# A routed-experts block without its last stage: base rows sorted beside the shared expert, finished rows scattered by the blocks

## The reference

```python
x = x + ga * attn(h)                                   # x3 in the kernel
h = _layernorm(x) * (1 + cb) + sb
logits = h @ w_router.T                                # 16 experts, top 1
masked_inputs = sigmoid(top logit) * h                 # to the chosen expert alone
gate, up = split(masked_inputs @ gate_up_proj[e])      # 128 -> 2 x 256
expert_out = (up * silu(gate)) @ down_proj[e]          # 256 -> 128
shared = (silu(h @ w_gate.T) * (h @ w_up.T)) @ w_down.T
x = x + gb * (shared + expert_out)
```

## Time and profile before

| | |
|---|---|
| median of three runs | 394.68 us (393.13 to 394.87) |
| profiled execution | 393.6 us, its span 391.8 us |
| busy: PE, DVE, ACT, POOL | 296.8, 244.0, 179.3, 187.6 us (76, 62, 46, 48% of the span) |
| mean granted clock of the tensor engine | 0.858 |
| chain that ended last, by engine | PE 30%, DVE 24%, POOL 21%, issue 13%, ACT 7%, DMA 3% |
| DMA | 28,184 packets, 25.22 MB, mean 64 GB/s |

### The profile page before, as it was taken

How to read it: one execution, slowest core, us unless ns; L and a number is a source line. 1 busy time by engine, 2 the same in 40 slices (tenths; PEclk the granted TensorE clock), 3 DMA queues, 4 the chain that set the end, 5 groups by cost and what they waited for, 6 DMA issues and landing times.

```text
span 391.8 us, 4364 instructions
## 1 busy us (share of the span) xinstructions
PE 296.8 (76%) x1140; PEld 171.7 (44%) x1140; DVE 244.0 (62%) x514; ACT 179.3 (46%) x436; POOL 187.6 (48%) x267
## 2 busy tenths in 40 slices
PE   4363667877668766877795586699989999999844
PEld 4223234334433534544453343334436666666532
DVE  5148596997989889789688342634335444444423
ACT  2541654947556666555372543222214444444300
POOL 4542726558678485656273534310003666666610
PEclk9956598996998888767889598699999999999955
DMA  6688000102011010010010100132002222222057
GB/s 182 175 241 321 28 0 4 51 0 60 22 47 35 0 54 29 0 41 21 0 49 8 41 14 14 50 97 49 0 1 56 75 75 82 71 77 71 4 155 274
DMA packets 28184, 25.22 MB, mean 64 GB/s; under 512 B 3682, under 2 KB 21734, under 8 KB 28160
## 3 DMA queue, kind: packets, MB, share of 16 engines
q1 hardware_dynamic: 24480, 18.57, 16.5%
q0 software_dynamic: 2528, 4.27, 3.4%
q10 hardware_dynamic: 1152, 2.10, 1.4%
HBM read 17.42 MB, written 8.49 MB: 66 GB/s over the span
## 4 chain that ended last, share of the span: by engine, by line
PE 30%; DVE 24%; POOL 21%; issue 13%; ACT 7%; DMA 3%; SPq 0%; POOLq 0%; DVEq 0%; ACTq 0%
PE bank L858 23%; POOL y_rows L423 11%; PE bank L862 5%; DVE work L524 4%; POOL sorted_rows L400 4%; POOL work L377 3%; ACT work L724 2%; DMA work<-y_rows 2%; DVE work L543 2%; DVE work L519 2%; DVE work L517 1%; DVE work L541 1%; PE bank L901 1%; POOL work L381 1%; DVE work L528 1%
## 5 line engine op out<-in xcount | busy, mean ns | idle before, releaser
L423 POOL DMA_INDIRECT y_rows<-work x47 | 46.2, 982 | 71.2 <-ACT work L838 41.9
L862 PE MATMUL bank<-ident,work 128*128 128x128 f32 x192 | 40.2, 362 | 52.9 <-ACT work L724 23.9
L862 PEld LDWEIGHTS bank<-ident,work 128*128 128x128 f32 x192 | 29.9, 185 | 75.0 <-ACT work L724 28.9
L858 PE MATMUL bank<-up_experts,work 128*128 x94 | 48.2, 595 | 0.0
L685 DVE COPY work<-bank 128x256 f32<-128x256 f32 x47 | 19.9, 424 | 37.7 <-PE bank L1043 37.7
L400 POOL DMA_INDIRECT sorted_rows<-rows,slot_i x32 | 36.5, 1140 | 14.4 <-issue 8.9
L858 PE MATMUL bank<-work,Fk 128*128 128x512 f32 x64 | 34.9, 652 | 5.7 <-DVE work L506 5.7
L724 ACT ACTIVATE work<-work 128x128 f32<-128x128 f32 x64 | 26.3, 487 | 23.5 <-POOL work L381 23.5
L375 POOL TENSOR_SCALAR work<-work 128x4 f32<-128x4 f32 x32 | 6.7, 210 | 59.5 <-DVE work L432 58.6
L377 POOL TENSOR_TENSOR work<-work,neghalf 128x4 f32<-128x4 f32 x32 | 33.2, 1038 | 2.7
L858 PE MATMUL bank<-work,Fv 128*128 128x512 f32 x64 | 33.3, 648 | 0.0
(11 more groups left out here) (161 smaller groups left out, 630.4 us busy)
## 6 DMA issues: line engine op xcount, KB each, us to landing
up_experts<-in_gate_up SPq DMA_DIRECT2D x2, 2048.0 KB, 11.7
work<-sorted_rows SPq DMA_DIRECT2D x47, 66.0 KB, 1.8
work<-in_x SPq DMA_DIRECT2D x8, 256.0 KB, 3.4
work<-in_xT SPq DMA_DIRECT2D x8, 256.0 KB, 3.1
work<-y_rows SPq DMA_DIRECT2D x8, 256.0 KB, 4.2
out_t<-work ACTq DMA_DIRECT2D x8, 256.0 KB, 3.9
sorted_rows<-pad_row SPq DMA_DIRECT2D x17, 66.0 KB, 1.6
y_rows<-work POOLq DMA_INDIRECT x47
```

The costliest lines, as they stand in the source:

```text
L423: pool.indirect_dma_start(y_rows, bass.IndirectOffsetOnAxis(number[q], 0), yb[q], None, bounds_check=NB * T - 1, oob_is_err=False).then_in ...
L858: return pe.matmul(out, w, x, start=start, stop=stop)
L862: last = pe.transpose(out[:, j * P:(j + 1) * P], src[:, j * P:(j + 1) * P], ident[:])
```

## The change

The gates gb are turned into rows with one row for all partitions (gb_rows): eight products against the identity matrix before the main loop, two ScalarE copies, and four transfers that put them into the second 128 columns of `rows`. A sorted row so carries h, gb and the number (260 values instead of 132). GpSimd makes one copy of the down weights per batch, multiplied by gb (`scale_down`, 128 x 256), after each batch's scatter. ScalarE keeps x3 as rows (from the transpose that the norm reads), `shared_down` multiplies in the other orientation (eight matmuls of 128 columns) so that its result is rows, and `shared_base` adds x3. GpSimd scatters these base rows into `sorted_base`, in the experts' order (32 indirect DMAs). Pads of both tensors are written, with a spare number each, behind the tensors' ends, and copied or written at each expert's end.

In the blocks, SyncE loads the sorted rows and the base rows of each block; the first three loads of rows stand ahead of the wait for the base scatters (C_out). Numbers, gate times result, and the addition of the base are VectorE's (`expert_y`, signal D_y); the copy of aT moves from VectorE to ScalarE; the buffers are 8 deep instead of 6. GpSimd scatters finished rows to out_t, which now is tokens by channels with spare rows at its end. The last stage is gone.

```diff
-    ROW = C + 4
+    ROW = 2 * C + 4
+    NUM = 2 * C
     ROOM = NB * T + P
     PADS = E * ROOM
-    NOROW = NB * T
+    SPARE = NBLK - NTT
     LAG = 3
-    DEPTH = 6
-    ENDS = 4
+    DEPTH = 8
+    LEAD = 3
...
+        x3_rows = sb("x3_rows", [P, NB, T])
+        gb_rows = sb("gb_rows", [P, NB, C])
+        Wd_gb = sb("Wd_gb", [P, NB, FC, C])
...
+            sp.wait_ge(K_gb.sem, K_gb.after(0))
+            for j in range(NT):
+                sp.dma_start(rows[:].rearrange("p (b j) r -> p b j r", j=NT)[:, :, j, C:2 * C], gb_rows[:]).then_inc(L_gb.sem, 16)
...
+            pads = sorted_rows[PADS:, :].rearrange("(k p) r -> p k r", p=P)
+            sp.dma_start(pads[:, :, 0:NUM], pad_row[:].rearrange("p (o r) -> p o r", o=1).broadcast_to([P, SPARE + E, NUM])).then_inc(L_pads.sem, 16)
+            sp.dma_start(pads[:, :, NUM:], pad_id[:]).then_inc(L_pads.sem, 16)
+            sp.dma_start(sorted_base[PADS:, :].rearrange("(k p) c -> p k c", p=P),
+                         pad_row[:, 0:C].rearrange("p (o c) -> p o c", o=1).broadcast_to([P, SPARE, C])).then_inc(L_pads.sem, 16)
...
-                sp.dma_start(sorted_rows[bass.ds(at_row, P), :], pad_row[:]).then_inc(L_pads.sem, 16)
+                sp.dma_start(sorted_rows[bass.ds(at_row, P), :], sorted_rows[PADS + (SPARE + e) * P:PADS + (SPARE + e + 1) * P, :]).then_inc(L_pads.sem, 16)
+                sp.dma_start(sorted_base[bass.ds(at_row, P), :], pad_row[:, 0:C]).then_inc(L_pads.sem, 16)
...
+            def load_rows(j):
+                q = j % DEPTH
+                at_row = block_row(j)
+                if j >= DEPTH:
+                    sp.wait_ge(D_y.sem, D_y.after(j - DEPTH))
+                sp.dma_start(xb[q], sorted_rows[bass.ds(at_row, P), :]).then_inc(D_x[q].sem, 16)
...
+            for j in range(LEAD):
+                load_rows(j)
+            sp.wait_ge(C_out.sem, C_out.after(NB - 1))
             for j in range(NBLK):
...
+                if block_no(j + LEAD):
+                    load_rows(j + LEAD)
+                load_base(j)
...
+            def scale_down(b):
+                if b == 0:
+                    pool.wait_ge(L_shared.sem, L_shared.after(0))
+                    pool.wait_ge(K_gb.sem, K_gb.after(0))
+                pool.tensor_tensor(Wd_gb[:, b], Wd[:], gb_rows[:, b:b + 1, :].broadcast_to([P, FC, C]), ALU.mult).then_inc(C_scale.sem, 1)
...
+                if batch(s - 1):
+                    scale_down(s - 1)
+
+            for b in range(NB):
+                pool.wait_ge(C_base.sem, C_base.after(b))
+                for j in range(NT):
+                    pool.indirect_dma_start(sorted_base, bass.IndirectOffsetOnAxis(slot_i[:, b * NT + j:b * NT + j + 1], 0),
+                                            x3_rows[:, b, j * C:(j + 1) * C], None).then_inc(C_out.sem, 16)
 
             for j in range(NBLK):
                 q = j % DEPTH
                 pool.wait_ge(D_y.sem, D_y.after(j))
-                pool.indirect_dma_start(y_rows, bass.IndirectOffsetOnAxis(number[q], 0), yb[q], None,
-                                        bounds_check=NB * T - 1, oob_is_err=False).then_inc(D_out[q].sem, 16)
...
+                pool.indirect_dma_start(out_t, bass.IndirectOffsetOnAxis(number[q], 0), yb[q], None).then_inc(D_out[q].sem, 16)
...
-                x3 = x3_all[:, span(b, T)]
-                dve.scalar_tensor_tensor(x3, bank[shared_banks[b % 2][0]][:], modc[:, GB, b:b + 1], x3,
-                                         ALU.mult, ALU.add).then_inc(C_base.sem, 1)
+                dve.tensor_tensor(x3_rows[:, b], bank[shared_banks[b % 2][0]][:], x3_rows[:, b], ALU.add).then_inc(C_base.sem, 1)
...
             def expert_act(j):
                 q = j % DEPTH
+                dve.wait_ge(D_sg.sem, D_sg.after(j))
+                dve.tensor_tensor(acte[j % 2], sge[j % 2], bank[2 + j % 2][:, F:2 * F], ALU.mult).then_inc(D_act.sem, 1)
+
+            def expert_y(j):
+                q = j % DEPTH
                 if j >= DEPTH:
                     dve.wait_ge(D_out[q].sem, D_out[q].after(j // DEPTH - 1))
-                dve.wait_ge(D_sg.sem, D_sg.after(j))
-                dve.tensor_copy(number[q], xb[q][:, C:C + 1].bitcast(I32)).then_inc(D_act.sem, 1)
-                dve.tensor_tensor(acte[j % 2], sge[j % 2], bank[2 + j % 2][:, F:2 * F], ALU.mult).then_inc(D_act.sem, 1)
-
-            def expert_aT(j):
-                dve.wait_ge(D_at.sem, D_at.after(j))
-                dve.tensor_copy(aT[j % 2], bank[4 + j % 2][:, 0:F]).then_inc(D_aT.sem, 1)
-
-            for s in range(NBLK + 2):
-                if block_no(s - 2):
-                    expert_aT(s - 2)
+                dve.tensor_copy(number[q], xb[q][:, NUM:NUM + 1].bitcast(I32)).then_inc(D_y.sem, 1)
+                dve.wait_ge(D_dn.sem, D_dn.after(j))
+                dve.tensor_tensor(yb[q], bank[6 + j % 2][:, 0:C], xb[q][:, C:2 * C], ALU.mult).then_inc(D_y.sem, 1)
+                dve.wait_ge(D_y.sem, D_y.after(j, 2))
+                dve.wait_ge(D_base[q].sem, D_base[q].after(j // DEPTH))
+                dve.tensor_tensor(yb[q], yb[q], xbase[q], ALU.add).then_inc(D_y.sem, 1)
+
+            for s in range(NBLK + 3):
                 if block_no(s - 1):
                     expert_act(s - 1)
-
-            for b in range(NB):
...
-                dve.scalar_tensor_tensor(fin[q], bank[q][:], modc[:, GB, b:b + 1], x3_all[:, span(b, T)],
-                                         ALU.mult, ALU.add).then_inc(E_f.sem, 1)
...
-                act.wait_ge(A_x3.sem, A_x3.after(b))
-                act.copy(x3_all[:, span(b, T)], x3w).then_inc(A_keep.sem, 1)
+                act.wait_ge(A_st[3].sem, A_st[3].after(b))
+                act.copy(x3_rows[:, b], bank[bT3][:]).then_inc(A_keep.sem, 1)
...
-            def expert_y(j):
-                q = j % DEPTH
-                act.wait_ge(D_dn.sem, D_dn.after(j))
-                if j >= DEPTH:
-                    act.wait_ge(D_out[q].sem, D_out[q].after(j // DEPTH - 1))
-                act.copy(yb[q], bank[6 + j % 2][:, 0:C]).then_inc(D_y.sem, 1)
-
-            for s in range(NBLK + 3):
+            def expert_aT(j):
+                act.wait_ge(D_at.sem, D_at.after(j))
+                act.copy(aT[j % 2], bank[4 + j % 2][:, 0:F]).then_inc(D_aT.sem, 1)
+
+            for s in range(NBLK + 2):
+                if block_no(s - 2):
+                    expert_aT(s - 2)
                 if block_no(s):
                     expert_xT(s)
                 if block_no(s - 1):
                     expert_silu(s - 1)
-                if block_no(s - 3):
-                    expert_y(s - 3)
...
+            for b in range(NB):
+                last = mm(bank[5 + b // NT][:, b % NT * C:(b % NT + 1) * C], modc[:, GB, b:b + 1].broadcast_to([P, P]), ident[:])
+                if b % NT == NT - 1:
+                    last.then_inc(K_gbm.sem, 1)
...
-                for c in range(FC):
-                    last = mm(bank[shared_banks[q][0]][:], Wd[:, c], sg[q][c], start=c == 0, stop=c == FC - 1)
+                pe.wait_ge(C_scale.sem, C_scale.after(b))
+                for j in range(NT):
+                    for c in range(FC):
+                        last = mm(bank[shared_banks[q][0]][:, j * C:(j + 1) * C], sg[q][c][:, j * P:(j + 1) * P], Wd_gb[:, b, c],
+                                  start=c == 0, stop=c == FC - 1)
...
-                    pe.wait_ge(D_y.sem, D_y.after(j - 2))
+                    pe.wait_ge(D_y.sem, D_y.after(j - 2, 2))
...
-            for b in range(NB):
...
-                turn(bank[q], flat(yt[q])).then_inc(E_t.sem, 1)
...
+    out_t = nc.dram_tensor("out_t", (nb * nt + (2 * ne - 1) * 128, c), mybir.dt.float32, kind="ExternalOutput").ap()
```

More of the change, by code:

```diff
@@ L719, in _, with gb_copy @@
             modulation_rows(0)
+            def gb_copy(n):
+                act.wait_ge(K_gbm.sem, n + 1)
+                act.copy(gb_rows[:, n * NT:(n + 1) * NT, :], tok(5 + n)).then_inc(K_gb.sem, 1)
             def norm_rows(done, n, b, src, dst):
```

84 lines of the change are left out of this document (37 added, 47 removed).

## The result

The changed kernel takes 418.72 us (median of four runs, 417.41 to 420.32) against 394.77 us for the kernel before beside it (393.13 to 396.01): a ratio of 1.0611 (95% interval 1.0557 to 1.0665), 6.1% slower. I had forecast 405.5 with a range of 393.5 to 413: the direction was right, the size was not, and the range did not hold it. The profiled execution has a span of 416.9 us, 25.1 more than before.

A forecast was written before the change was run, and what follows sets the result against it. The tensor engine, fully busy at 1.634 us per block iteration, was taken as the bound. -17.0 + 15.2 + 9.0 + 1.6 + 2.2 + 0.3 = +11.3 us gave 403.1 on the span; forecast 405.5, range 393.5 to 413.

The forecast's parts named there:

- What goes: End of the kernel: everything behind the last block's rows landing goes, as the last scatter writes the output; -17.0 us.
- The ring: Block loop: waits through turn, aT, xT and gate_up set a period of 1.98 us, not 1.634; +15.2 us.
- To the tensor engine: 0.06: Block loop: the link from the end of ScalarE's xT copy to the tensor engine's gate_up, taken as 0.06 us.
- The restart: Start of the blocks: the fourth block's rows wait until all 32 base scatters have landed; +9.0 us.
- The clock: First blocks after the seven-microsecond wait: the tensor engine runs at half rate for 4 us; +1.6 us.
- the rival by which it does not hold: Blocks: short waits drop the clock, a tenth or fifth of iterations at half rate; 411 or 417 us, chance 0.15.
- The main loop: Main loop +2.2 us from three scale_downs at 0.72 on the chain of waits; prologue's gate rows +0.3.
- Pads and SyncE's issues: Small pads hidden in the shared expert, large pads 0 or a few us, two SyncE issues per block (1.64) hidden.
- The drain of the pipeline: After the blocks' last turn: two VectorE output steps for one of ScalarE, no queue of scatters; 0.
- tail: End of the kernel: the stretch behind the last rows' landing, 391.8 - 374.75, counted as saved; -17.0 us.
- The first rival: Block loop: xT is out in time and the period stays 1.634 us; -3.9, 390 us, chance 0.12.
- the second (hidden restart): Start of the blocks: base scatters end with the shared expert, 9.0 and 1.6 go; +0.7, 395 us, chance 0.08.

The follow-up runs named there:

- e1_order: The changed kernel with ScalarE's block-loop order turned to xT, silu, aT in place of aT, xT, silu; 403.55 us.
- e8_before_ring: The kernel before, with only the block loop's aT copy moved to ScalarE ahead of xT and silu, and y's copy to VectorE; 415.32 us, ratio 1.0626.
- e9_hold_fixed: The changed kernel with eight blocks' rows loaded ahead of the base-scatter wait, early base adds held later, base loads running four blocks ahead; 412.27 us.
- c1: The changed kernel itself, unedited, measured once more on chip 12; 424.98 us.

## Why the prediction was wrong

**The step that failed** is "What goes": "All behind that landing: 391.8 - 374.75 = 17.0 us. After the change the last scatter writes the output itself." 8.9 went (19.2 to 10.3 behind the last scatter's start). The output is in place 2.2 us after the scatter's start, as I had it, but GpSimd's list ends in a drain that takes 0.082 us for each indirect DMA queued, and the sum had nothing for it. In the kernel before the last stage hid it; with that stage gone it is the last thing to end, and the change made it longer: 79 x 0.082 = 6.5 became 111 x 0.082 = 9.1. That is 8.1 of the 13.8 us missed on the span. For the largest term of the sum I looked at the end of the data and not at the end of each engine's list.

**The ring** was right in mechanism (e1_order, e8_before_ring) and mis-sized: the link "To the tensor engine: 0.06" was taken from VectorE's product and the weight load that it releases; from ScalarE's xT to gate_up it is 0.14. With that link the period is 2.055, not 1.98: 44 x 0.075 = 3.3 us, and 0.8 at the first turn, for which the sum had nothing, so 19.3 instead of 15.2.

**The restart** was right: +8.7 against 9.0. The base scatters were spaced 1.26 as taken, and landing, SyncE and the load's landing came within 0.2 of what was put down for them; the first scatter starts 0.28 behind its base, not 0.77. **The clock** fell as said and cost 0.6, not 1.6. It did not fall in the blocks: the rival by which it does not hold came nearest to the measured total (411 to 417) by a wrong road. **The main loop** was +5.1 up to row_in(0), not 2.2 + 0.3: I counted three scale_downs on the chain of waits at 0.72. In the trace after four stand there, at 0.80 with their gaps, but their sum of 3.2 is no account of the 5.1, since nearly all of it is there after the first of them (table above); the cause stays open. Pads and SyncE's issues were hidden in the first measurement, as said: the x load behind the large pads is 5.4 late, the one ahead of them already 5.0, and the 32 small ones took 28 us of issues, not 19, and still ended before the blocks. **The drain of the pipeline** was +0.3 against 0.

By terms: tail 8.1, ring 4.1, main loop 2.6, restart and clock -1.3, pipeline 0.3, together 13.8, the difference between 25.1 and 11.3. The first rival (no ring) and the second (hidden restart) were refuted by the trace; e1_order and e9_hold_fixed, which undo one and most of the other, gave 403.6 and 412.3, both above the kernel before, where I had 390 and 395. Much of that is the same missing 8.1.

The range was too narrow because every term in it but the tail had two bounds; the tail, the largest gain, stood in the sum as a fact. Its bounds were in the trace: nothing behind the landing, or the 5.4 us by which GpSimd's drain passes it even in the kernel before (380.1 against 374.75).

## What to carry to other kernels

Before a last stage is counted as saved, look up what ends on each engine's own list behind it: queue drains and waits that it hid come to light, at their full length. A step moved from one engine to another costs by where it stands in the new list: a copy placed ahead of one that the critical engine waits for can close a ring round it, and cost 16 to 19 us in 47 blocks, with VectorE, ScalarE and GpSimd half idle. And a loader's list must not put a load that is wanted now behind one whose buffer is not yet free.

## What the hardware did that I had not expected

GpSimd's drain at the end of the program takes 0.082 us for every indirect DMA since the last drain (47, 79 and 111 of them: 3.9, 6.5 and 9.15 us past the last scatter), down to a floor of 1.9 with 15 of them. A drain placed where GpSimd idles takes its share away (4.8 us for two); one placed among the blocks took 3.2 to 4.0 us for 16 scatters, and the kernels with two of them were not faster.

The sets of runs differ for one kernel and not for another, and the sets differ in their chips. The changed kernel took 418.7 us in the first measurement and 425.0 on chip 12, a descendant 390.5 and 405.2, and the kernel before 391 to 395 on all. In the slower cases VectorE stalls one to three times in the shared expert's stage, the longest time for 4.9 to 8.1 us and labelled "remote", while SyncE's 32 small pad transfers (16 of them from DRAM to DRAM) and GpSimd's scatters are in flight. SyncE is held in the same stretches: in c1's first stall three of its pad transfers in a row start 1.4 to 2.4 us behind the one before, where in the first measurement one gap of 1.4 is the longest. All ten kernels of the new kind on chips 7 and 12 had it, and none of the six on chips 3 and 11. Chip 7 had it in both of its sets; the other chips had one each, so that chip and set cannot be told apart there. The kernel e8_before_ring, of the old kind with 16 such transfers, all from SBUF, ran on chip 7 without it. What the stall is stays open: the pads were not taken out by themselves.

Two of SyncE's three large pad transfers held its queue for long: the pads' numbers (pieces of 16 bytes) and the base's pads (512 bytes) took 8.9 and 7.9 us to issue, where the first and largest (pieces of 1,024 bytes) took 0.43 and a plain load 0.35. Whether that is their small pieces or their place behind the first is not shown. It cost next to nothing here: the next x load comes 8.6 us after the second of them, and the two x loads around the pads stand at 174.06 and 200.41, where the kernel before, with one small pad transfer in place of the three, has them at 169.03 and 195.04.

```profile
174.44 0.43 SPq L313 DMA_DIRECT2D sorted_rows<-pad_row  x1
174.92 8.88 SPq L314 DMA_DIRECT2D sorted_rows<-pad_id  x1
183.84 7.94 SPq L315 DMA_DIRECT2D sorted_base<-pad_row  x1
200.41 0.35 SPq L280 DMA_DIRECT2D work<-in_xT  x1
```
